# Moving the relu between the two query/key projections ahead of the same slot's exponential on ScalarE

## The chip, the core and the metric

The kernel runs on one core of a Trainium2 chip. The metric is the device time of one execution in microseconds (us); before the change it is 1559.29 us, the median of three runs that lie between 1557.75 and 1560.46 us.

## What is computed

The input is 32 images of 128 channels by 56 x 56 pixels, float32. A first layer normalises each image in groups of 4 channels, gates every channel by a small deformable convolution over the channel means and adds the result to the image. The second layer is a local attention over the result, and it is where nearly all the time goes:

```python
value = _conv1x1(x, v_w, v_b)
keyf  = _proj(x, k1_w, ..., k2_w, ...)      # 1x1 conv, batch norm, relu, twice
query = _proj(x, q1_w, ..., q2_w, ...)      # the same with other weights
uk = concatenate([_unfold3(keyf, d) for d in (1, 2, 4)])
uv = concatenate([_unfold3(value, d) for d in (1, 2, 4)])
sim = softmax(sum(uk * query))              # 27 neighbours of each pixel
out = _conv1x1(sum(sim * uv), w_w, w_b)
```

`_proj` is the part that the change touches: `h = relu(W1 x + b1)`, then `relu(W2 h + b2)`. Queries and keys are made together, 64 channels each, stacked to 128 rows.

## The kernel before

An image is cut into 7 vertical strips, 8 pixels wide, of 448 pixels each. A strip is 7 units of 8 x 8 pixels, and two units together (128 pixels) are a **tile** of the attention; an image has 25 tiles. For a tile the scores against the 256 pixels around it are one matrix product; a mask keeps the neighbours that count.

The program of each engine is written out as a list of **slots**, one for each image n and tile t, 32 x 25 of them after a ramp. The engines run through their lists in order and wait for each other by semaphores. In slot t the work of several tiles stands side by side, each at another stage:

- TensorE (PE): the scores of tile t (L416, into ps_s), the transposes of tile t-3 (L428, into ps_t), in some slots a first projection (L466, into ps_p) and the values (L489, into ps_v), then the context products of tile t-5 (L449 and L454, into ps_o), in some slots a second projection (L471, into ps_p), and small products of the normalisation of a later image.
- VectorE (DVE): the reciprocal of tile t-1's sum (L937), mask and minimum of tile t (L929), the scaling of tile t-1 (L943 or L946), statistics and small steps for later images (L982 to L1028, with L1008 waiting for GpSimd's hat_sum), the final sum of a finished strip (L954), and the values' bias (L967).
- ScalarE (ACT): the copy of a pair of transposed tiles out of PSUM (L599, into eT; every second slot), the exponential of tile t with its row sum (L584), in some slots the relu after the first projection (L634, into hid), in some slots keys and queries (L621 into kk, L610 into qq), and now and then a step for a later image (L645, L650).

The projections of the next image are laid over the current one by a table, `G_SLOT = [-10, -6, -3, 1, 4, 8, 11]`: entry g is the slot, counted from the strip's own image's slot 0, in which strip g is projected. Negative entries are the slots 15, 19 and 22 of the image ahead. So in slots 15, 19, 22, 1, 4, 8 and 11 of every image PE does a first projection and ACT the relu, and in the slot after each, 16, 20, 23, 2, 5, 9 and 12, PE does the second projection, and ACT the keys and queries.

The waits that matter here are these. The relu waits for the first projection (`h_ps`); the second projection waits for the relu (`h_done`); keys and queries wait for the second projection (`qk_ps`). The exponential of tile t waits for its masked scores (`z_done`), and the next reciprocal on DVE, which stands ahead of the mask of tile t+1, waits for the exponential (`e_done`). The context products of tile t-5 wait for the copies into eT (`eT_done`). The scores of tile t wait for the mask of tile t-2, since ps_s has two banks. ps_p and hid are single buffers.

Of the kernel before, what the change touches and what calls it, by code (L numbers as in the profile page):

```python
# [46 lines left out]
G_SLOT = [-10, -6, -3, 1, 4, 8, 11]  # L47
# [14 lines left out]
def half_tile(h):  # L62

    return divmod(h, UNITS)


def last_tile(s):

    return (UNITS * s + UNITS - 1) // 2
# [75 lines left out]
def lagged(n, t, lag):  # L145

    return (n, t - lag) if t >= lag else (n + -1, t - lag + TILES)


def slots(first, last, drain=0, register=None):  # L150

    for o in range(first, last + 1):
        for t in range(TILES):
            yield Image(o, register), t
    for t in range(drain):
        yield Image(last + 1, register), t


def build(nc, x, par, w1, w2, wv, wo, bo, bv, wg, out):
    with ExitStack() as ctx:  # L160
# [141 lines left out]
        def items_at(n, t):  # L302

            for m, rel in ((n, t), (n + 1, t - TILES)):
                if m.exists():
                    yield m, rel

        def chain_at(n, t):

            for m, rel in ((n + 1, t + TILES), (n + 2, t), (n + 3, t - TILES)):  # L310
                if m.exists():
                    yield m, rel
# [7 lines left out]
        def col(c, n=1):  # L320
            return g1[:, c:c + n]

        def images(first, last, drain=0, register=None):

            with nc.Block() as block:
# [244 lines left out]
                @block.scalar  # L570
                def _(act):
                    act.wait_ge(v_zero, 2)
                    for to in (qq[:].rearrange("p a b -> p (a b)"), kk[:].rearrange("p a b -> p (a b)"),
                               xb[:, PAIRS - 1, CHUNKS // 2, 1, :]):
                        nc.scalar.activation(to, zero[:].to_broadcast([P, to.shape[1]]),
                                             ACT.Copy).then_inc(a_zero, 1)
                    act.wait_ge(g_zs, 1)
                    act.wait_ge(a_zero, 2)

                    def exponentials(n, t):  # L580
                        i = t % RING
                        act.wait_ge(z_done.sem, z_done.count(n, t + 1))
                        act.wait_ge(rz_done.sem, rz_done.count(n, t + 1 - RING))
                        nc.scalar.activation(e[:, i, :], e[:, i, :], ACT.Exp, bias=zmin[:, i:i + 1], scale=-1.0,  # L584
                                             accum_out=zs[:, i:i + 1]).then_inc(e_done.next(), 1)

                    def copy(n, j):
                        last = min(2 * j + 1, TILES - 1)
                        act.wait_ge(t_done.sem, t_done.count(n, last + 1))

                        h = 4 * j
                        s = half_tile(h)[0]
                        if s >= ESTRIPS:
                            act.wait_ge(c_done.sem, c_done.count(n, 2 * j + 2 - ESTRIPS * UNITS // 2))
                        else:
                            act.wait_ge(c_done.sem, c_done.count(n + -1, min(TILES, 2 * j + 2 + ESTRIPS * UNITS // 2)))
                        base = 2 * UPIX * (h % (ESTRIPS * UNITS))
                        size = 4 * 2 * UPIX if last == 2 * j + 1 else 2 * UPIX
                        nc.scalar.activation(eT[:, base:base + size], ps_t[(EPAIRS * n.parity() + j) % 2][:, 0:size],  # L599
                                             ACT.Copy).then_inc(eT_done.next(), 1)  # L600

                    def queries(m, g):
                        act.wait_ge(qk_ps.sem, qk_ps.count(m, g + 1))
                        act.wait_ge(s_done.sem, s_done.count(m + -1, last_tile(g) + 1))
                        src = ps_p[0:HD, 0:SPIX].rearrange("p (u k) -> p u k", k=UPIX)
                        first = UNITS * g // 2
                        for b in range(2):
                            units = range((b + g) % 2, UNITS, 2)
                            at = (UNITS * g + units[0]) // 2
                            last = nc.scalar.activation(  # L610
                                qq[HD * b:HD * (b + 1), at:at + len(units), UPIX * b:UPIX * (b + 1)],
                                src[:, units[0]:UNITS:2, :], ACT.Relu, bias=bn_t[0:HD, 1:2])
                        last.then_inc(q_done.next(), 1)

                    def keys(m, g):
                        act.wait_ge(qk_ps.sem, qk_ps.count(m, g + 1))
                        act.wait_ge(s_done.sem, s_done.count(m + -1, last_tile(min(g + 1, STRIPS - 1)) + 1))
                        a = kk[0:HD, g, HALO * SIDE + HALO:HALO * SIDE + HALO + 1]
                        to = bass.AP(a.tensor, a.offset, [list(a.ap[0]), [BPIX - HALO, 2], [SIDE, H], [1, HALO]])
                        src = ps_p[HD:P, 0:SPIX].rearrange("p (r h c) -> p h r c", h=2, c=HALO)  # L620
                        nc.scalar.activation(to, src, ACT.Relu, bias=bn_t[HD:P, 1:2]).then_inc(k_done.next(), 1)  # L621

                    def slot(n, t):
                        m, k = lagged(n, t, TRANSPOSE)
                        if m.exists() and (k % 2 == 1 or k == TILES - 1):
                            copy(m, k // 2)
                        if n.exists():
                            exponentials(n, t)
                        for m, rel in items_at(n, t):
                            for g, at in enumerate(G_SLOT):  # L630
                                if rel == at:
                                    act.wait_ge(h_ps.sem, h_ps.count(m, g + 1))
                                    act.wait_ge(qk_ps.sem, qk_ps.count(m, g))
                                    nc.scalar.activation(hid[:], ps_p[:, 0:SPIX], ACT.Relu,  # L634
                                                         bias=b1x[:, m.parity():m.parity() + 1]).then_inc(h_done.next(), 1)
                                if rel == at + 1:
                                    keys(m, g)
                                    queries(m, g)
                        for m, at in chain_at(n, t):
                            if at == CH["a4"]:  # L640

                                act.wait_ge(dg.sem, dg.count(m, 10))
                                act.wait_ge(pg.sem, pg.count((m + -1), 13))
                                for k in range(TAPS):
                                    nc.scalar.activation(hats[:, k, 0, :], iota_f[:], ACT.Abs, bias=col(POS + k),  # L645
                                                         scale=-1.0).then_inc(ag.next(), 1)
                            if at == CH["a6"]:

                                act.wait_ge(dg.sem, dg.count(m, 11))
                                nc.scalar.activation(col(EX), col(ZS), ACT.Exp, bias=nbd[:, 0:1],  # L650
                                                     scale=-1.0).then_inc(ag.next(), 1)

                    for n, t in slots(first, last, drain, register):
                        slot(n, t)
# [436 lines left out]
```

## Time and profile before

| | |
|---|---|
| median of 3 runs | 1559.29 us (1557.75 to 1560.46) |
| the profiled execution's own time | 1560.12 us |
| its span, first to last instruction | 1558.4 us |
| granted TensorE clock, mean | 0.997 of full speed |
| busy, share of the span | PE 95%, PE weight loads 78%, DVE 77%, ACT 75%, POOL 49% |
| DMA | mean 132 GB/s |

Time of the profiled execution outside its span is 1560.12 - 1558.4 = 1.7 us. An engine's busy time counts instructions that compute; waiting is the idle time ahead of an instruction, and the view of waits names the instruction that ended it. The matmuls of this kernel are recorded in two rows each, and a timeline row merges instructions of one group that follow each other; a duration of such a row includes the end of the pipeline, so the distance between the starts of two rows says more than the durations.

### The profile page before, as it was taken

To read this page: it belongs to the slowest core of one execution; us is meant where nothing else is said; L and a number is where in the kernel's file an instruction comes from. 1 tells how busy PE (TensorE), PEld (TensorE's weight loads), DVE (VectorE), ACT (ScalarE), POOL (GpSimd) and SP (SyncE) were. 2 spreads that over 40 slices of the span, in tenths; PEclk is the share of its full clock that TensorE was granted. 3 is DMA by queue.
4 is the path that set the end of the run, shared out by engine and by line. 5 is a ranking of instruction groups with operands and counts; after the bars stand their busy time and mean duration, and the time that the engine had idled before them with its cause. 6 is when DMAs were issued, how large, how long until landed. Compare 5 with 4: busy or idle time off the path is not lost.

```text
span 1558.4 us, 35493 instructions
## 1 busy us (share of the span) xinstructions
PE 1485.3 (95%) x9287; PEld 1208.7 (78%) x9287; DVE 1204.3 (77%) x4620; ACT 1166.1 (75%) x3044; POOL 771.1 (49%) x2194
## 2 busy tenths in 40 slices
PE   1899999999999999999999999999999999999998
PEld 1588777878777778778778778778778778778886
DVE  6487778777777877778777778877778877778776
ACT  2477777777777777777777777777777777777775
POOL 6454455554455454455454555454555454555430
PEclk9999999999999999999999999999999999999999
DMA  3144553444543444553444543444543444543334
GB/s 130 37 114 150 156 159 109 137 115 148 157 140 122 135 123 147 159 144 117 134 124 147 159 143 118 136 123 146 160 141 117 137 124 146 159 143 116 97 82 137
DMA packets 104276, 205.98 MB, mean 132 GB/s; under 512 B 13584, under 2 KB 83600, under 8 KB 95888
## 3 DMA queue, kind: packets, MB, share of 16 engines
q1 hardware_dynamic: 104080, 203.72, 43.8%
q8 instruction: 80, 1.31, 0.4%
q14 instruction: 116, 0.95, 0.2%
HBM read 51.62 MB, written 51.38 MB: 66 GB/s over the span
## 4 chain that ended last, share of the span: by engine, by line
PE 72%; POOL 9%; issue 7%; DVE 6%; ACT 5%; DMA 1%; SPq 0%; ACTq 0%; POOLq 0%; DVEq 0%
PE ps_s L416 17%; PE ps_o L449 13%; PE ps_p L471 10%; PE ps_v L489 10%; PE ps_t L428 8%; PE ps_p L466 8%; POOL hats L752 5%; PE ps_o L454 2%; ACT hid L634 2%; POOL hats L751 2%; DVE e L929 1%; ACT e L584 1%; DVE e L946 1%; POOL hat_sum L755 1%; DVE rz L937 1%
## 5 line engine op out<-in xcount | busy, mean ns | idle before, releaser
L584 ACT ACTIVATE e<-e,zmin 128x256 f32<-128x256 f32 x800 | 404.4, 506 | 237.2 <-DVE zmin L929 229.4
L929 DVE CUSTOM_DVE_ANT_0 e<-ps_s,mask 128x256 f32<-128x256 f32 x800 | 334.3, 418 | 136.4 <-PE ps_s L416 129.7
L449 PEld LDWEIGHTS ps_o<-eT,v 128*128 128x128 f32 x2688 | 377.8, 191 | 74.2 <-issue 69.6
L449 PE MATMUL ps_o<-eT,v 128*128 128x128 f32 x2688 | 433.9, 276 | 0.5 <-ACT eT L599 0.3
L416 PE MATMUL ps_s<-kk,qq 128*128 128x256 f32 x1408 | 428.1, 386 | 1.5 <-DVE zmin L929 1.5
L428 PE MATMUL ps_t<-ident,e 128*128 128x128 f32 x1600 | 306.0, 273 | 0.2 <-DVE e L946 0.2
L428 PEld LDWEIGHTS ps_t<-ident,e 128*128 128x128 f32 x1600 | 225.3, 141 | 81.1 <-DVE e L946 0.5
L599 ACT ACTIVATE eT<-ps_t 128x512 f32<-128x512 f32 (+1 forms) x416 | 234.2, 563 | 48.9 <-PE ps_t L428 46.4
L416 PEld LDWEIGHTS ps_s<-kk,qq 128*128 128x128 f32 x1408 | 221.3, 192 | 37.7 <-issue 29.2
L946 DVE SCALAR_TENSOR_TENSOR e<-e,rz,keep 128x256 f32<-128x256 f32 x480 | 245.8, 512 | 0.1
L471 PE MATMUL ps_p<-hid,w2T 128*128 128x448 f32 x448 | 216.9, 566 | 27.4 <-ACT hid L634 25.8
L489 PE MATMUL ps_v<-wvox,xb 128*128 128x128 f32 x1600 | 216.9, 276 | 0.8 <-DVE v L967 0.8
L489 PEld LDWEIGHTS ps_v<-wvox,xb 128*128 128x128 f32 x1600 | 200.5, 193 | 14.6 <-issue 13.5
L937 DVE RECIPROCAL rz<-zs 128x1 f32<-128x1 f32 x800 | 124.9, 156 | 109.7 <-ACT e L584 108.4
L466 PE MATMUL ps_p<-raw,w1x 128*128 128x448 f32 x448 | 207.7, 546 | 0.9 <-ACT qq L610 0.8
L733 POOL TENSOR_TENSOR g<-g,mhalf 128x1 f32<-128x1 f32 x64 | 36.4, 569 | 340.1 <-DVE g L995 241.3
L610 ACT ACTIVATE qq<-ps_p,bn_t 64x256 f32<-64x256 f32 (+1 forms) x448 | 198.1, 442 | 8.4
L800 POOL TENSOR_SCALAR raw<-raw,g 128x448 f32<-128x448 f32 x224 | 165.0, 739 | 35.2 <-PE ps_p L466 35.2
L621 ACT ACTIVATE kk<-ps_p,bn_t 64x448 f32<-64x448 f32 x224 | 141.4, 631 | 50.1 <-PE ps_p L471 37.6
L751 POOL TENSOR_SCALAR hats<-hats 128x128 f32<-128x128 f32 x96 | 30.8, 320 | 252.7 <-ACT hats L645 247.1
L634 ACT ACTIVATE hid<-ps_p,b1x 128x448 f32<-128x448 f32 x224 | 138.3, 617 | 17.3 <-PE ps_p L466 17.2
L584 ACT ACTIVATION_READ_ACCUMULATOR e<-e,zmin 128x1 f32 x800 | 150.4, 188 | 0.0
(147 smaller groups left out, 1927.6 us busy)
## 6 DMA issues: line engine op xcount, KB each, us to landing
raw<-in_x_dram SPq DMA_DIRECT2D x32, 1568.0 KB, 7.3
out_dram<-raw SPq DMA_DIRECT2D x32, 1568.0 KB, 5.4
v<-v SPq DMA_DIRECT2D x192, 224.0 KB, 3.2
kk<-kk SPq DMA_DIRECT2D x192, 112.0 KB, 2.2
ksp<-kk SPq DMA_DIRECT2D x192, 64.0 KB, 2.5
v<-v_last SPq DMA_DIRECT2D x64, 128.0 KB, 2.9
kk<-kk SPq DMA_DIRECT2D x32, 224.0 KB, 2.9
v<-v_last SPq DMA_DIRECT2D x64, 96.0 KB, 2.7
```

What stands on the lines that cost most here:

```text
L416: nc.tensor.matmul(ps_s[i][:, 0:KEYS].rearrange("p (s h k) -> p h s k", s=2, h=2), qq[:, t, :], window.rearrange("p h (s k) -> p h s k", s=2),
L428: last = nc.tensor.transpose(o[:, base:base + KEYS].rearrange("p (a s k) -> p s a k", a=2, s=2)[:, i], e[:, t % RING, P * i:P * (i + 1)], ...
L449: last = nc.tensor.matmul(o[:, UPIX * (u - 1):UPIX * (u + 1)], v[:, s, u, :], eT[:, UPIX * (base + 2 * u - 1):UPIX * (base + 2 * u + 1)], ...
L466: nc.tensor.matmul(ps_p[:, 0:SPIX].rearrange("p (r c) -> p r c", c=SIDE), w1x[:, m.parity(), :], strip_of(m, g), start=True, stop=True).th ...
L471: nc.tensor.matmul(ps_p[:, 0:SPIX], w2T[:], hid[:], start=True, stop=True).then_inc(qk_ps.next(), 1)
L489: last = nc.tensor.matmul(ps_v[:, P * j:P * (j + 1)], pixels, wvox[:, m.parity(), :], start=True, stop=True)
L584: nc.scalar.activation(e[:, i, :], e[:, i, :], ACT.Exp, bias=zmin[:, i:i + 1], scale=-1.0, accum_out=zs[:, i:i + 1]).then_inc(e_done.next( ...
L599: nc.scalar.activation(eT[:, base:base + size], ps_t[(EPAIRS * n.parity() + j) % 2][:, 0:size], ACT.Copy).then_inc(eT_done.next(), 1)
L610: last = nc.scalar.activation(qq[HD * b:HD * (b + 1), at:at + len(units), UPIX * b:UPIX * (b + 1)], src[:, units[0]:UNITS:2, :], ACT.Relu, ...
L634: nc.scalar.activation(hid[:], ps_p[:, 0:SPIX], ACT.Relu, bias=b1x[:, m.parity():m.parity() + 1]).then_inc(h_done.next(), 1)
L929: nc.vector.tensor_tensor_reduce(e[:, i, :], ps_s[(TILES * n.parity() + t) % 2][:, 0:KEYS], mask[:].rearrange("p s h a b -> p (s h a b)"), ...
L946: nc.vector.scalar_tensor_tensor(e[:, i, :], e[:, i, :], rz[:, i:i + 1], keep[:, KINDS.index(outside(t)), :], ALU.mult, ALU.mult).then_inc ...
```

## The change

In ACT's slot the relu between the two projections is issued ahead of the exponential of the same slot. The copy before it, and the keys and queries behind it, stay where they were. No instruction is added or removed, and the other engines' lists are the same.

```diff
                         if m.exists() and (k % 2 == 1 or k == TILES - 1):
                             copy(m, k // 2)
-                        if n.exists():
-                            exponentials(n, t)
                         for m, rel in items_at(n, t):
                             for g, at in enumerate(G_SLOT):
                                 if rel == at:
                                     act.wait_ge(h_ps.sem, h_ps.count(m, g + 1))
                                     act.wait_ge(qk_ps.sem, qk_ps.count(m, g))
                                     nc.scalar.activation(hid[:], ps_p[:, 0:SPIX], ACT.Relu,
                                                          bias=b1x[:, m.parity():m.parity() + 1]).then_inc(h_done.next(), 1)
+                        if n.exists():
+                            exponentials(n, t)
+                        for m, rel in items_at(n, t):
+                            for g, at in enumerate(G_SLOT):
                                 if rel == at + 1:
                                     keys(m, g)
                                     queries(m, g)
```

Two lines are added to the file above L634, so lines behind them have other numbers in the changed kernel: the relu is L632 there, the steps L645 and L650 are L647 and L652.

ACT's list from slot 21 to slot 24 of image 0, before (e, zs is the exponential of a tile, hid the relu, eT the copy, kk and qq the keys and queries, hats a step for a later image):

```order
L584 ACTIVATE e,zs<-e,zmin 128x256
L645 ACTIVATE hats<-iota_f,g 128x128 x3
L599 ACTIVATE eT<-ps_t 128x512
L584 ACTIVATE e,zs<-e,zmin 128x256
L634 ACTIVATE hid<-ps_p,b1x 128x448
L584 ACTIVATE e,zs<-e,zmin 128x256
L621 ACTIVATE kk<-ps_p,bn_t 64x2x56x4
```

And with the change:

```order
L584 ACTIVATE e,zs<-e,zmin 128x256
L647 ACTIVATE hats<-iota_f,g 128x128 x3
L599 ACTIVATE eT<-ps_t 128x512
L632 ACTIVATE hid<-ps_p,b1x 128x448
L584 ACTIVATE e,zs<-e,zmin 128x256 x2
L621 ACTIVATE kk<-ps_p,bn_t 64x2x56x4
```

In slot 22 the relu now follows the copy at once, and the exponential of tile 22 comes behind it, directly ahead of that of tile 23.

Slots 1 and 2 of the image after, ACT, before:

```order
L599 ACTIVATE eT<-ps_t 128x512
L584 ACTIVATE e,zs<-e,zmin 128x256
L634 ACTIVATE hid<-ps_p,b1x 128x448
L599 ACTIVATE eT<-ps_t 128x128
L584 ACTIVATE e,zs<-e,zmin 128x256
```

And with the change:

```order
L599 ACTIVATE eT<-ps_t 128x512
L632 ACTIVATE hid<-ps_p,b1x 128x448
L584 ACTIVATE e,zs<-e,zmin 128x256
L599 ACTIVATE eT<-ps_t 128x128
L584 ACTIVATE e,zs<-e,zmin 128x256
```

Here the relu of strip 3 and the exponential of tile 1 have changed places. The other five slots with a relu change in the same way.

## Rows read from the trace of the kernel before

**Rows 1.** The page's first part: busy us, share of the span, instructions

```profile
PE 1485.3 (95%) x9287; PEld 1208.7 (78%) x9287; DVE 1204.3 (77%) x4620; ACT 1166.1 (75%) x3044; POOL 771.1 (49%) x2194
```

**Rows 2.** View of waits, whole span: us in total, times, longest us

```profile
DVE e L929 <- PE ps_s L416: 129.7, 255, 2.1
...
PEld ps_p L471 <- ACT hid L634: 41.9, 66, 2.2
...
PE ps_p L471 <- ACT hid L634: 25.8, 36, 1.8
```

**Rows 3.** Timeline, PE, slot 20 of one image: start us, us, instruction, count, [idle]

```profile
707.09 0.61 PE L449 MATMUL ps_o<-eT,v 128*128 128x128 f32 x4
707.54 0.92 PE L471 MATMUL ps_p<-hid,w2T 128*128 128x448 f32 x2
```

**Rows 4.** Timeline, all engines, slots 15 and 16, rows of PE and ACT

```profile
743.97 0.92 PE L466 MATMUL ps_p<-raw,w1x 128*128 128x448 f32 x2
...
745.31 0.51 ACT L584 ACTIVATE e<-e,zmin 128x256 f32<-128x256 f32 x1 [0.65 <-DVE zmin L929]
...
745.82 0.61 PE L449 MATMUL ps_o<-eT,v 128*128 128x128 f32 x4
746.48 1.02 PE L471 MATMUL ps_p<-hid,w2T 128*128 128x448 f32 x2
```

**Rows 5.** Timeline, PE, slots 23 to 2 around an image's start

```profile
712.78 0.61 PE L449 MATMUL ps_o<-eT,v 128*128 128x128 f32 x4
713.24 1.02 PE L471 MATMUL ps_p<-hid,w2T 128*128 128x448 f32 x2
...
716.52 0.71 PE L449 MATMUL ps_o<-eT,v 128*128 128x128 f32 x4
...
717.95 0.92 PE L466 MATMUL ps_p<-raw,w1x 128*128 128x448 f32 x2
...
719.58 0.61 PE L449 MATMUL ps_o<-eT,v 128*128 128x128 f32 x4
720.91 1.02 PE L471 MATMUL ps_p<-hid,w2T 128*128 128x448 f32 x2 [0.72 <-ACT hid L634]
```

**Rows 6.** Timeline, all engines, slots 19, 20 and 23, rows of ACT and DVE

```profile
705.69 0.51 ACT L584 ACTIVATE e<-e,zmin 128x256 f32<-128x256 f32 x1 [1.16 <-DVE zmin L929]
...
706.20 0.63 ACT L634 ACTIVATE hid<-ps_p,b1x 128x448 f32<-128x448 f32 x1
...
707.07 0.42 DVE L929 CUSTOM_DVE_ANT_0 e<-ps_s,mask 128x256 f32<-128x256 f32 x1 [0.55 <-PE ps_s L416]
...
712.85 0.42 DVE L929 CUSTOM_DVE_ANT_0 e<-ps_s,mask 128x256 f32<-128x256 f32 x1
```

**Rows 7.** Timeline, ACT, slots 22 to 2

```profile
711.60 0.58 ACT L599 ACTIVATE eT<-ps_t 128x512 f32<-128x512 f32 x1
712.08 0.50 ACT L584 ACTIVATE e<-e,zmin 128x256 f32<-128x256 f32 x1
...
712.57 0.62 ACT L634 ACTIVATE hid<-ps_p,b1x 128x448 f32<-128x448 f32 x1
713.32 0.51 ACT L584 ACTIVATE e<-e,zmin 128x256 f32<-128x256 f32 x1
...
714.30 0.63 ACT L621 ACTIVATE kk<-ps_p,bn_t 64x448 f32<-64x448 f32 x1 [0.38 <-PE ps_p L471]
...
715.87 0.60 ACT L599 ACTIVATE eT<-ps_t 128x512 f32<-128x512 f32 x1
...
719.73 0.51 ACT L584 ACTIVATE e<-e,zmin 128x256 f32<-128x256 f32 x1 [0.77 <-DVE zmin L929]
...
720.24 0.61 ACT L634 ACTIVATE hid<-ps_p,b1x 128x448 f32<-128x448 f32 x1
720.76 0.27 ACT L599 ACTIVATE eT<-ps_t 128x128 f32<-128x128 f32 x1
```

## The prediction

> **What bounds the kernel now.** I read the page's busy shares first. PE is busy for 95% of the span, ACT and DVE for 75% and 77% [rows 1]. So PE is the engine to follow, and a change on ACT is worth what it takes out of PE's waits or puts into them.
>
> The view of waits says who makes PE wait. The second projection (L471) waits for the relu (L634) 36 times for 25.8 us, and its weight load 66 times for 41.9 us [rows 2]; 36 + 66 = 102 events are about three in each of 32 images. In the other direction DVE waits 129.7 us for PE's scores [rows 2]: over a whole image the softmax loop on DVE and ACT has time to spare, about 129.7 / 32 = 4.1 us.
>
> The timeline then tells which three slots these are, and what each costs. Seen in slot 20, where nothing waits, the second projection starts 707.54 - 707.09 = 0.45 us after the four context products ahead of it [rows 3]. Against this I hold the slots that do wait:
>
> - Slot 16: 746.48 - 745.82 = 0.66 us [rows 4], 0.21 late.
> - Slot 23: 713.24 - 712.78 = 0.46 us, 0.01 late.
> - Slot 2: 720.91 - 719.58 = 1.33 us, 0.88 late [rows 5].
>
> In all three the second projection's row is also 1.02 us long and not 0.92 [rows 3 to 5]: its weights could not be loaded ahead of time, and I count the 0.10 us as PE time too. That makes 0.31, 0.11 and 0.98 us, **1.40 us of PE time per image**. In slots 5, 9, 12 and 20 the projection does not wait, so an earlier relu gives nothing there.
>
> **The change part by part.** Nothing is added or removed; on ACT a relu and an exponential change places in seven slots per image. ACT issues no DMA, so no queue is passed.
>
> *The relu, earlier.* It can start when its first projection is over and ACT is free.
> Slot 15: the first projection ends at 743.97 + 0.92 = 744.89, and ACT is idle from 745.31 - 0.65 = 744.66 [rows 4]. The relu, 0.62 us long [rows 7], is over by 745.55; the second projection is wanted at 745.82 + 0.45 = 746.27. The 0.31 us go entirely. From here PE leads by 0.31.
> Slot 22: the relu takes the place of the exponential at 712.08 and is over at 712.70 instead of 713.19 [rows 7]. With PE 0.31 ahead the projection is wanted at 713.23 - 0.31 = 712.92. The 0.11 us go; the lead is 0.42.
> Slot 1: the first projection ends at 717.95 + 0.92 = 718.87 [rows 5], ACT is idle from 719.73 - 0.77 = 718.96 [rows 7]. The relu could be over by 719.6 instead of 720.85, and the projection is wanted at 719.58 + 0.45 = 720.03 on the old clock. Here the relu waited for an exponential that itself waited for DVE. The 0.98 us go.
>
> *The exponential, later.* A relu pushes what stands behind it by 720.76 - 720.24 = 0.52 us [rows 7], plus any time that ACT now idles until the projection is over.
> Slot 19 is the bad one. The exponential runs at 705.69, while PE is still in the first projection, and the relu follows at 706.20 [rows 6]. Swapped, the relu stays where it is, or 0.31 earlier with PE's lead, at 705.89, and the exponential comes at 706.41 instead of 705.69, 0.72 later. The next mask on DVE, where it waits for nothing else, follows an exponential after 712.85 - 712.08 = 0.77 us [rows 6, 7], so here at 707.18. It stood at 707.07, having waited 0.55 for PE [rows 6]. That slack hides all but 0.11 us.
> Slot 22: copy and relu come 0.1 late, the exponential of tile 22 at 712.08 + 0.10 + 0.52 = 712.70. The next one follows after 713.32 - 712.08 = 1.24 us [rows 7], a round of exponential, reciprocal, mask, exponential: at 713.94. Keys come 712.57 - 712.08 = 0.49 behind it [rows 7], at 714.43. They stood at 714.30, where they waited for the second projection [rows 7]; that is no longer what ends last. The keys, the queries and the copy of the next pair into eT keep their distance of 715.87 - 714.30 = 1.57 us [rows 7], so the copy starts at 716.00, 0.13 later than before.
> **That copy is what is late next.** The context products of slot 0 start at 716.52, 0.65 behind it, and their row is 0.71 us against 0.61 elsewhere [rows 3, 5]: they already wait for it a little. PE arrives there with a lead of 0.42 and now finds the copy 0.13 later than before: the lead is lost, and 0.13 with it, 0.55 us in all.
> Slot 1 then has everything 0.13 later: the first projection ends at 719.00, the relu at about 719.66, and the second projection is wanted at 720.16. It still doesn't wait.
> Slots 4, 8, 11 and 15: the exponential there moves by 0.5 to 0.6 us at most, and the next mask is one that waits for PE's scores, as in slot 20 (0.55 us [rows 6]); I cost them at nothing. If that cover is thinner than in slot 20, each costs up to 0.1 us, as slot 19 does.
>
> *The sum.* 1.40 - 0.55 = 0.85 us per image. Of the 32 images the first starts in the ramp and the last has no next image to project; I count 30, so 0.85 x 30 = 25 us. The profiled execution took 1560.12 us and would take 1535; it stands 0.8 us above the median of the runs, so the forecast is 1559.3 - 25 = **1534 us**.
>
> The uncertain term is the 0.55. Its lower end is 0: if keys still follow the second projection directly, the copy moves with PE and nothing is lost. Its upper end, from the rows, is a full 0.72 of slot 19 and 0.62 of slot 22 passed on, 1.34 at the copy, plus the lead of 0.42: 1.76. I take 0.55, near the lower end, because the wait in slot 20 that hides most of the 0.72 is in the rows.
>
> The relu's 0.62 us and 0.52 to the next start are this trace's [rows 7]. The Trainium skill's page "ScalarE: Activation LUTs", section "What ACT_TABLE_LOAD costs", gives an ACTIVATE with a per-partition bias about 280 ns + 0.833 ns per element and an overlap of 93 ns with the next: an estimate from it is 653 ns for 448 elements and 0.56 us to the next start. By that each push would be 0.04 us longer, the copy 0.08, and the sum 2.4 us smaller, 1536 us; the rows are measured here and decide.
>
> **The rivals.**
>
> *All of it comes out.* If the late exponentials are caught up before slot 0, the full 1.40 x 30 = 42 us are gained: 1517 us. For it: the 4.1 us per image that DVE waits. Against: the copy ahead of slot 0 is reached by the chain of slots 19 to 24, where only slot 20 has a wait to give.
>
> *The wait turns into another and the time stays, or gains little.* PE meets a later copy, or scores whose mask is late, and gives back 1 to 1.4 of the 1.40 us: 1547 to 1559 us. The Trainium skill speaks for this in "Perfetto Trace Analysis", section "Identifying the Most-Contended Engine": matmul busy time is no good measure of how full TensorE is, the weight loads' share is better, and that share is 78% here [rows 1], no more than DVE's. By that rule the loop on DVE and ACT would set the pace and the time would stay at 1559 us. The 129.7 us that DVE waits for PE [rows 2] speak against it.
>
> *Slower: ACT stands idle in front of a relu while a ready exponential waits behind it.* The place is slot 19, 0.72 us, followed by slot 22, 0.62. If both reach the copy before slot 0, PE loses 1.76 and gains 1.40: 0.36 x 30 = 11 us, 1570 us. It decides from 1.40 - 0.42 = 0.98 us of delay at the copy on. For it: ACT is strictly in order, and the mask of the next tile stands behind the reciprocal that needs the exponential. Against: the 0.55 us in slot 20.
>
> That the relu isn't earlier at all is true in slot 19 alone, where it starts at the projection's end already.
>
> **How the numbers follow.** The forecast, with the 0.55 off by 0.25 either way (1526 to 1542 us), has 0.55. All of it, down to 1515, has 0.13. A small gain, 1542 to 1556, has 0.12. No change has 0.09, slower 0.11. A measurement of this kernel tells about 0.2%, 3 us, from no change, so faster is 0.55 + 0.13 + 0.12 = 0.80. The range from 1515 to 1556 us leaves out no change and slower, 0.20. The likeliest case's own range is 1526 to 1542.
>
> **What would show it.** In the profile after, the wait of the second projection for the relu should be nearly gone, 41.9 and 25.8 us down to a few. PE's context products of slot 0 should wait for the copy into eT, about 0.5 us per image, some 15 us in all where there were almost none. The exponential should stand behind the relu in seven slots, and DVE's wait for PE's scores should fall by 10 us or more, most of it in slot 20. Keys in slot 23 should wait for ACT's exponential and no longer for PE. I am wrong if the scores (L416) or transposes (L428) start to wait for DVE, or if the relu still ends last in slot 2.

## The result, and the profile after

The changed kernel takes **1550.8 us** (median of 6 runs, 1548.23 to 1555.5) and the kernel before, beside it, 1559.88 us (6 runs, 1557.75 to 1560.97). The ratio is 0.9945 with a 95% interval of 0.9934 to 0.9956. So 9.1 us are gained where 25 were forecast: the sign was right, the size was not, and 1550.8 lies inside the range only through the case "a small gain".

The page's first part of the changed kernel, whose profiled execution took 1550.79 us with a span of 1549.1 us at the same granted clock of 0.997:

```profile
PE 1481.5 (96%) x9287; PEld 1203.9 (78%) x9287; DVE 1198.9 (77%) x4620; ACT 1175.4 (76%) x3044; POOL 779.1 (50%) x2194
```

The busy times moved by about 1% at most against [rows 1]; the gain is waiting time. The view of waits of the changed kernel (us in total, times, longest us):

```profile
DVE rz L939 <- ACT e L584: 192.4, 352, 1.6
...
DVE e L931 <- PE ps_s L416: 42.7, 97, 1.1
...
PEld ps_o L449 <- ACT eT L599: 24.0, 38, 0.7
...
PE ps_o L449 <- ACT eT L599: 14.9, 30, 0.5
...
PEld ps_p L466 <- ACT qq L610: 12.9, 33, 0.9
...
PEld ps_p L471 <- ACT hid L632: 5.0, 4, 2.1
...
PE ps_p L471 <- ACT hid L632: 2.2, 4, 0.7
```

The wait for the relu is all but gone: 41.9 and 25.8 us in [rows 2], 5.0 and 2.2 now. Two waits have come in its place. The context products (L449) wait for the copy into eT, 30 times 0.5 us. And the first projection's weight load (L466) waits 33 times for the queries (L610), 31 of them in slot 4, once per image; that one stood in no row of the prediction. DVE waits 42.7 us for PE's scores where it was 129.7 [rows 2], and in exchange longer for the exponential, 192.4 us (108.4 before).

To see where in an image the time went, I take the distance from the start of one scores row (L416) on PE to the next as the length of a slot, and the median over images 2 to 28. An image fell from 46.73 to 46.42 us, by 0.32 of unrounded times; 0.32 x 30 = 9.6 us, close to the 9.1 us measured. All the difference lies in five slots:

| slot | before | after | difference | forecast |
|---|---|---|---|---|
| 16 | 2.17 | 1.85 | -0.31 | -0.31 |
| 23 | 1.97 | 1.90 | -0.07 | -0.11 |
| 0 | 1.43 | 2.09 | +0.66 | +0.55 |
| 2 | 2.98 | 1.99 | -0.99 | -0.98 |
| 4 | 2.74 | 3.13 | +0.39 | 0 |

These slots can be read off one image. Timeline of PE in the kernel before, slots 0 to 4 (start us, us, instruction, count); the five starts of scores bound slots 0, 1, 2 and 4:

```profile
715.86 0.60 PE L416 MATMUL ps_s<-kk,qq 128*128 128x256 f32 x2
...
717.30 0.60 PE L416 MATMUL ps_s<-kk,qq 128*128 128x256 f32 x2
...
718.92 0.60 PE L416 MATMUL ps_s<-kk,qq 128*128 128x256 f32 x2
...
721.90 0.68 PE L416 MATMUL ps_s<-ksp,qq 128*128 128x256 f32 x2
...
723.08 0.60 PE L416 MATMUL ps_s<-kk,qq 128*128 128x256 f32 x2
723.52 0.38 PE L428 MATMUL ps_t<-ident,e 128*128 128x128 f32 x2
723.74 0.92 PE L466 MATMUL ps_p<-raw,w1x 128*128 128x448 f32 x2
...
725.83 0.60 PE L416 MATMUL ps_s<-kk,qq 128*128 128x256 f32 x2
```

The timeline of the same image after, PE and its weight loads, from slot 23 on:

```profile
708.62 0.61 PE L449 MATMUL ps_o<-eT,v 128*128 128x128 f32 x4
709.07 0.97 PE L471 MATMUL ps_p<-hid,w2T 128*128 128x448 f32 x2
...
711.64 0.60 PE L416 MATMUL ps_s<-kk,qq 128*128 128x256 f32 x2
712.08 0.38 PE L428 MATMUL ps_t<-ident,e 128*128 128x128 f32 x2
712.96 0.71 PE L449 MATMUL ps_o<-eT,v 128*128 128x128 f32 x4 [0.50 <-ACT eT L599]
...
713.73 0.60 PE L416 MATMUL ps_s<-kk,qq 128*128 128x256 f32 x2
...
715.36 0.60 PE L416 MATMUL ps_s<-kk,qq 128*128 128x256 f32 x2
...
717.35 0.68 PE L416 MATMUL ps_s<-ksp,qq 128*128 128x256 f32 x2
...
718.53 0.60 PE L416 MATMUL ps_s<-kk,qq 128*128 128x256 f32 x2
718.97 0.38 PE L428 MATMUL ps_t<-ident,e 128*128 128x128 f32 x2
719.48 0.30 PEld L466 LDWEIGHTS ps_p<-raw,w1x 128*128 128x128 f32 x2 [0.37 <-ACT qq L610]
719.48 1.02 PE L466 MATMUL ps_p<-raw,w1x 128*128 128x448 f32 x2
...
721.67 0.60 PE L416 MATMUL ps_s<-kk,qq 128*128 128x256 f32 x2
```

Slot 2 is now 717.35 - 715.36 = 1.99 us instead of 2.98. Slot 0 is 713.73 - 711.64 = 2.09 instead of 1.44, with the wait for eT inside. In slot 4 the first projection starts 719.48 - 718.97 = 0.51 us behind the transposes; before it was 723.74 - 723.52 = 0.22. Its weights come late as well, so its row is 1.02 us long and not 0.92: 0.29 + 0.10 = 0.39 us, the slot's whole loss. With the distance between the two traces at the scores of slot 14 as zero, PE's lead in this image is 0.31 us after slot 16, 0.37 at the start of slot 0, minus 0.28 after it, 0.70 after slot 2 and 0.30 after slot 4.

The gain of slot 16, on PE of the next image (before: [rows 4]):

```profile
741.66 0.61 PE L449 MATMUL ps_o<-eT,v 128*128 128x128 f32 x4
742.11 0.92 PE L471 MATMUL ps_p<-hid,w2T 128*128 128x448 f32 x2
```

The second projection starts 0.45 us behind the context products and its row is 0.92 us long, as in a slot where nothing waits.

ACT's timeline after, of the same image, tells whom PE waits for:

```profile
702.03 0.64 ACT L632 ACTIVATE hid<-ps_p,b1x 128x448 f32<-128x448 f32 x1 [1.66 <-PE ps_p L466]
702.57 0.50 ACT L584 ACTIVATE e<-e,zmin 128x256 f32<-128x256 f32 x1
...
708.35 0.61 ACT L632 ACTIVATE hid<-ps_p,b1x 128x448 f32<-128x448 f32 x1
708.87 0.50 ACT L584 ACTIVATE e<-e,zmin 128x256 f32<-128x256 f32 x1
...
710.11 0.51 ACT L584 ACTIVATE e<-e,zmin 128x256 f32<-128x256 f32 x1 [0.65 <-DVE zmin L931]
...
710.73 0.63 ACT L621 ACTIVATE kk<-ps_p,bn_t 64x448 f32<-64x448 f32 x1
...
712.31 0.60 ACT L599 ACTIVATE eT<-ps_t 128x512 f32<-128x512 f32 x1
...
717.25 0.51 ACT L584 ACTIVATE e<-e,zmin 128x256 f32<-128x256 f32 x1 [0.57 <-DVE zmin L931]
...
717.87 0.63 ACT L621 ACTIVATE kk<-ps_p,bn_t 64x448 f32<-64x448 f32 x1
718.53 0.90 ACT L610 ACTIVATE qq<-ps_p,bn_t 64x192 f32<-64x192 f32 x2
```

In slot 19 (the first two rows) ACT stands idle for 1.66 us ahead of the relu, with the exponential behind it; the exponential's masked scores are complete at 701.49, 0.54 us before the relu starts. The keys of slot 23 follow the exponential of tile 23 (710.11) and no longer the projection, and the copy at 712.31 is the one that the context products of slot 0 wait for: 712.96 - 712.31 = 0.65, as before. The queries of strip 3 end at 718.53 + 0.90 = 719.43, and at 719.48 the first projection of strip 4 begins. It writes ps_p, the single buffer that the queries read; the queries stand behind the keys, and these behind the exponential of tile 2 at 717.25, which waited for DVE.

### The profile page after: what moved, and what is told of

The parts are those of the page before. It is cut to its first block, busy times and chain, and to the rows that moved or that the text cites. A ratio compares the mean times of both kernels' runs of the same rounds, so it can differ in the third digit from the quotient of the medians.

```text
span 1549.1 us, 35493 instructions
## 1 busy us (share of the span) xinstructions
PE 1481.5 (96%) x9287; PEld 1203.9 (78%) x9287; DVE 1198.9 (77%) x4620; ACT 1175.4 (76%) x3044; POOL 779.1 (50%) x2194
## 4 chain that ended last, share of the span: by engine, by line
PE 61%; DVE 13%; issue 10%; POOL 8%; ACT 7%; DMA 1%; SPq 0%; ACTq 0%; POOLq 0%; DVEq 0%
PE ps_s L416 14%; PE ps_o L449 12%; PE ps_p L466 9%; PE ps_v L489 8%; PE ps_t L428 7%; PE ps_p L471 6%; POOL hats L754 4%; PE ps_o L454 2%; DVE e L931 2%; ACT e L584 2%; POOL hats L753 2%; ACT hats L647 2%; DVE e L948 2%; DVE cells L1003 1%; ACT kk L621 1%
## 5 line engine op out<-in xcount | busy, mean ns | idle before, releaser
L449 PEld LDWEIGHTS ps_o<-eT,v 128*128 128x128 f32 x2688 | 377.8, 191 | 93.8 <-issue 69.6
L449 PE MATMUL ps_o<-eT,v 128*128 128x128 f32 x2688 | 434.1, 276 | 15.2 <-ACT eT L599 14.9
L416 PE MATMUL ps_s<-kk,qq 128*128 128x256 f32 x1408 | 428.1, 386 | 1.5 <-DVE zmin L931 1.5
L931 DVE CUSTOM_DVE_ANT_0 e<-ps_s,mask 128x256 f32<-128x256 f32 x800 | 333.9, 417 | 50.0 <-PE ps_s L416 42.7
L939 DVE RECIPROCAL rz<-zs 128x1 f32<-128x1 f32 x800 | 126.2, 158 | 193.6 <-ACT e L584 192.4
L599 ACT ACTIVATE eT<-ps_t 128x512 f32<-128x512 f32 (+1 forms) x416 | 234.9, 565 | 25.8 <-PE ps_t L428 23.3
L416 PEld LDWEIGHTS ps_s<-kk,qq 128*128 128x128 f32 x1408 | 221.3, 192 | 37.6 <-issue 29.4
L948 DVE SCALAR_TENSOR_TENSOR e<-e,rz,keep 128x256 f32<-128x256 f32 x480 | 237.4, 495 | 0.1
L632 ACT ACTIVATE hid<-ps_p,b1x 128x448 f32<-128x448 f32 x224 | 141.6, 632 | 110.8 <-PE ps_p L466 107.7
L466 PE MATMUL ps_p<-raw,w1x 128*128 128x448 f32 x448 | 211.3, 554 | 4.9 <-ACT qq L610 1.3
L471 PE MATMUL ps_p<-hid,w2T 128*128 128x448 f32 x448 | 209.1, 549 | 2.2 <-ACT hid L632 2.2
L610 ACT ACTIVATE qq<-ps_p,bn_t 64x256 f32<-64x256 f32 (+1 forms) x448 | 198.0, 442 | 8.4
L802 POOL TENSOR_SCALAR raw<-raw,g 128x448 f32<-128x448 f32 x224 | 171.8, 769 | 35.0 <-PE ps_p L466 35.0
```

What stands on the lines that cost most here:

```text
L416: nc.tensor.matmul(ps_s[i][:, 0:KEYS].rearrange("p (s h k) -> p h s k", s=2, h=2), qq[:, t, :], window.rearrange("p h (s k) -> p h s k", s=2),
L449: last = nc.tensor.matmul(o[:, UPIX * (u - 1):UPIX * (u + 1)], v[:, s, u, :], eT[:, UPIX * (base + 2 * u - 1):UPIX * (base + 2 * u + 1)], ...
L466: nc.tensor.matmul(ps_p[:, 0:SPIX].rearrange("p (r c) -> p r c", c=SIDE), w1x[:, m.parity(), :], strip_of(m, g), start=True, stop=True).th ...
L471: nc.tensor.matmul(ps_p[:, 0:SPIX], w2T[:], hid[:], start=True, stop=True).then_inc(qk_ps.next(), 1)
L610: last = nc.scalar.activation(qq[HD * b:HD * (b + 1), at:at + len(units), UPIX * b:UPIX * (b + 1)], src[:, units[0]:UNITS:2, :], ACT.Relu, ...
L802: gp.tensor_scalar(to, to, col(X_A + m.offset % RAWS), col(X_B + m.parity()), ALU.mult, ALU.add).then_inc(x1_done.next(), 1)
```

## The experiments

Three theories were set against each other.

- **A, two named waits.** The relu of slots 15 and 1 gives its full gain. What takes it back is (1) the exponentials of slots 19 and 22, pushed behind their relus, which make the copy ahead of slot 0 late, and (2) in slot 4 the queries that still hold ps_p, a wait that the late relu of slot 2 had covered.
- **B, the loop.** The softmax loop on DVE and ACT sets the pace, and any lead that PE wins is taken back somewhere.
- **C, the copies of keys.** PE ahead of time meets the DMA into ksp (the copy of the keys that some scores read) in slot 10.

All variants name the strips whose relu is issued first, and put the rest back behind the exponential. A variant's cut shows the lines in which it differs from the kernel before or from a variant already shown. Strips 0 to 6 stand for slots 15, 19, 22, 1, 4, 8 and 11:

```diff
+RELU_FIRST = (0, 3)
...
-                                if rel == at:
+                                    if rel == at and (g in RELU_FIRST) == where:
...
+                        relu(True)
                         if n.exists():
                             exponentials(n, t)
+                        relu(False)
+                        keys_queries(False)
```

The line numbers of the variants are 2 to 22 higher than in the changed kernel.

### Only slots 15 and 1

> The relu goes first in slots 15 and 1 alone (strips 0 and 3); in slots 19, 22, 4, 8 and 11 the exponential goes first, as before the change. Theory A (two named waits: the exponentials pushed in slots 19 and 22 make the copy into eT late in slot 0, and the first projection of slot 4 finds ps_p still read by the queries of slot 2): the context products of slot 0 no longer wait for the copy more than before; PE gains 0.31 + 0.98 us per image and gives back about 0.5 in slot 4: 0.8 x 30 = 24 us, 1535 us. Theory B (the softmax loop of DVE and ACT sets the pace, and PE's lead is taken back whichever slots are swapped): about the time of the change, 1550 us.

Measured: 1544.05 us, ratio 0.9896 (0.9883 to 0.9909) to 1560.27 us. The view of waits:

```profile
PEld ps_p L468 <- ACT qq L612: 20.4, 33, 0.9
...
PE ps_p L468 <- ACT qq L612: 12.4, 31, 0.8
...
PEld ps_o L451 <- ACT eT L601: 1.8, 6, 0.5
```

With slots 19 and 22 put back the wait for eT is gone (14.9 and 24.0 us in the changed kernel), and the time is better than the whole change's. But the loss in slot 4 grew from 0.39 to 0.66 us per image: the two waits had partly covered each other. In the changed kernel PE came out of slot 0 0.28 us late, and the exponential of tile 2, on which the queries hang, did not come later with it: it starts 25.82 us behind the scores of slot 14 there (median over images 2 to 28), 25.80 before the change. Here PE is not late, and the whole 0.66 shows. A's 1535 had 0.5 for it and was missed by 9 us, of which this is 5; B's 1550 was missed too.

### Only slots 19 and 22

```diff
-RELU_FIRST = (0, 3)
+RELU_FIRST = (1, 2)
```

> The relu goes first in slots 19 and 22 alone (strips 1 and 2). Theory A: nothing but the harm is left: the copy ahead of slot 0 comes about 0.45 us later than before the change and PE waits for it, less the 0.1 us of slot 23: 0.35 to 0.45 us per image, 10 to 13 us, 1570 us. Theory B: no place to gain, none to lose, 1557 to 1560 us.

Measured: 1569.31 us, ratio 1.0064 (1.0051 to 1.0077). The view of waits:

```profile
PEld ps_o L451 <- ACT eT L601: 23.2, 36, 0.7
...
PE ps_o L451 <- ACT eT L601: 14.7, 30, 0.5
```

The wait of slot 0 stands here alone, at the size that it has in the changed kernel, and slot 0 is 0.65 us longer. This half of the change is a loss of 9 us. B had no loss here.

### Only slot 1

```diff
-RELU_FIRST = (0, 3)
+RELU_FIRST = (3,)
```

> The relu goes first in slot 1 alone (strip 3). Theory A: 0.98 us gained in slot 2, about 0.55 given back in slot 4 by the first projection waiting for the queries: 0.4 x 30 = 13 us, 1547 us, and the row of that wait about 0.5 us per image. Theory B: PE's lead goes somewhere else too, 1555 to 1560 us.

Measured: 1549.16 us, ratio 0.9928 (0.9916 to 0.994). Slot 2 gains its 0.99 us and slot 4 gives 0.65 back, though slot 4's own relu stands where it stood before the change: the loss comes with PE's lead out of slot 2. B's 1555 to 1560 is missed. One moved relu of the seven is worth as much as all seven together.

### The whole change, and in slot 4 the values ahead of the first projection

To take away the wait in slot 4, PE does the value products, which don't touch ps_p, before the first projection of strip 4:

```diff
+VALUES_FIRST = (4,)
...
-                                if rel == at:
+                                if rel == at and g not in VALUES_FIRST:
                                     hidden(m, g)
                             if rel in V_SLOT:
                                 values(m, V_SLOT.index(rel))
+                            for g, at in enumerate(G_SLOT):
+                                if rel == at and g in VALUES_FIRST:
+                                    hidden(m, g)
```

> The change as it is, all seven slots swapped, and on PE in slot 4 the eight value products ahead of the first projection instead of behind it, so that the projection wants ps_p about 0.9 us later. Theory A: the wait for the queries goes and 0.39 us per image with it, 12 us against the change, 1539 us; the wait of slot 0 for the copy stays at 0.5 us. Theory B: the wait turns up in another place, 1550 us.

Measured: 1552.16 us, ratio 0.9956 (0.994 to 0.9972), no better than the change alone. The wait for the queries did go (1.4 us), but another came. The view of waits:

```profile
PEld ps_s L419 <- DMA ksp<-kk: 25.8, 33, 2.3
...
PE ps_s L419 <- DMA ksp<-kk: 11.0, 8, 1.7
```

In 6 of 27 images the scores of slot 10 wait some 1.5 us more for the keys' copy, and the mean image is 46.55 us long where the median is 46.25 (in the changed kernel 46.52 and 46.42). The relu of slot 4 stands ahead of the exponential here and comes later than in the changed kernel, since its projection does; it pushes the exponential, and the keys of strip 4 end 2.78 us behind the scores of slot 5 instead of 2.46. So the wait that C names is there, in one combination. That the later keys bring it is not shown: in those six images the copy takes 5.8 to 6.1 us from issue to landing, 4.1 in the median image, and such copies also occur where the keys are on time (slots 4, 8 and 11 alone, below).

### Slots 15 and 1, and in slot 4 the values first

```diff
+RELU_FIRST = (0, 3)
+VALUES_FIRST = (4,)
```

> The relu first in slots 15 and 1 alone, and on PE the value products of slot 4 ahead of its first projection. The run before it with seven slots swapped moved keys of strip 4 by 0.3 us, because the relu of slot 4, now later, pushed the exponential; here that relu stays behind the exponential. Theory A: the 0.66 us that slot 4 costs with these two slots swapped falls to 0.2 or less, and nothing else grows: 0.45 x 30 = 13 us against that run, 1530 us. Theory C (past slot 5 PE meets the transfer of the keys, ksp, which the scores of slot 10 wait for, so that slot 4's wait only protected it): 1542 to 1546 us, with the wait for ksp up by 10 us or more.

Measured: 1532.44 us, ratio 0.9823 (0.9806 to 0.9839) to 1560.06 us. With the relu of slot 4 left behind its exponential the copy of the keys is no obstacle: PE's weight loads wait 8.2 us for it in all (6.0 before the change), and C's 1542 us or more is missed. 27.6 us are gained, near the 25 that I had forecast for the whole change. Slot 4 is still 0.40 us longer than before, for a new reason. Its timeline:

```profile
708.24 0.38 PE L431 MATMUL ps_t<-ident,e 128*128 128x128 f32 x2
708.38 0.15 DVE L1033 TENSOR_TENSOR g<-g,ps_v 128x1 f32<-128x1 f32 x1
...
708.79 1.13 PE L492 MATMUL ps_v<-wvox,xb 128*128 128x128 f32 x8 [0.16 <-issue]
```

The values start 0.55 us behind the transposes. They write ps_v, and PE's program holds them until a step of the normalisation on DVE that reads ps_v (L1033) is over. The row names no instruction as releaser, but in every image from 2 to 28 they start 0.25 us behind the end of that step, while their distance from the transposes varies from 0.53 to 0.64. One buffer was exchanged for another.

### Only slot 19

> The relu first in slot 19 alone. The exponential of tile 19 is pushed by about 1.0 us, of which DVE's wait of 0.55 hides half: copy, relu and second projection of slots 22 and 23 come about 0.4 us later, PE waits there, nothing is gained: 0.4 x 30 = 12 us, 1571 us. If the push is hidden entirely: 1559 us.

```diff
+RELU_FIRST = (1,)
```

Measured: 1573.25 us, ratio 1.008 (1.0064 to 1.0096). The view of waits:

```profile
PEld ps_p L473 <- ACT hid L635: 54.8, 94, 2.2
```

The late exponential of slot 19 makes the next ones late, and the relu of slot 22, still behind its exponential, with them. The second projection of slot 23 waits for it: 41.9 us [rows 2] become 54.8, and slot 23 is 0.42 us longer.

### Only slot 22

> The relu first in slot 22 alone. PE gains 0.1 us in slot 23; the exponential of tile 22 is pushed by 0.62 us, the keys of slot 23 and the copy behind them by 0.13, and the context products of slot 0 wait 0.24 longer; slot 2's wait shrinks by the 0.13, since the exponential there does not move: about 0, 1557 to 1562 us. If the push is passed on whole: 0.6 us in slot 0, 1570 us or more.

```diff
+RELU_FIRST = (2,)
```

Measured: 1558.96 us, ratio 0.9991 (0.9979 to 1.0002): no change that can be told. Slot 0 loses 0.27 us; slots 2 and 23 give 0.25 and 0.11.

### Only slots 4, 8 and 11

> The relu first in slots 4, 8 and 11 alone. The prediction costs these at nothing: every slot of PE keeps its length, 1558 to 1562 us. If the cover there is thinner: up to 0.1 us per slot and image, 9 us in all, 1569 us.

```diff
+RELU_FIRST = (4, 5, 6)
```

Measured: 1563.44 us, ratio 1.002 (1.0011 to 1.0029), slower by 3.4 us where nothing was expected. No slot's median moves, but the mean image is 46.93 us against a median of 46.72. The view of waits:

```profile
PEld ps_s L418 <- DMA ksp<-kk: 8.9, 12, 1.8
...
PE ps_s L418 <- DMA ksp<-kk: 3.2, 3, 1.1
```

In 3 of the 27 images the scores of slot 10 wait 1.0 to 1.1 us for the copy of the keys, and slot 9 is 1.2 us longer by it: 3.7 us in all, the whole loss. Before the change the mean image is 46.81 against 46.73. The keys and the issue of the copy come at the same times as before; in these three images the copy lands after 5.9 to 6.0 us, where the longest was 5.0. Why is open, and one profiled execution can't tell whether the swap brings it.

### Slots 15 and 1, and in slot 4 the context products first

PE's slot 4 has three pieces besides scores and transposes: first projection, values, context products. The last two variants order them freely, here as context, values, first projection:

```diff
+LATE = (2, 1, 0)
...
+                        parts = (first_projections, value_products, contexts)
+                        for part in LATE if t == G_SLOT[4] else (0, 1, 2):
+                            parts[part]()
```

> The relu first in slots 15 and 1 alone, and on PE in slot 4 the order is context products, value products, first projection. In the run with the value products ahead slot 4 still cost 0.40 us, of which the value products' wait for a normalisation step on DVE, 0.3 us, is the larger part. The context products need 0.44 us and would cover it. Theory A: slot 4 costs 0.1 us or less: 0.3 to 0.4 x 30 = 9 to 12 us against that run, 1521 to 1523 us. Theory C (the transfer of ksp ends last in slot 10): 1530 us or more, the wait for ksp up by 8 us or more.

Measured: 1526.82 us, ratio 0.9769 (0.9755 to 0.9782) to 1561.57 us. Slot 4 has its old length again, though slot 5 loses 0.11. A's 1521 to 1523 is missed by 4 us: slot 5 makes 3.4 of it, and in 2 of 27 images the scores of slot 10 wait 1.0 us for the keys' copy.

And as context, first projection, values:

```diff
-LATE = (2, 1, 0)
+LATE = (2, 0, 1)
```

> The same with the order context products, first projection, value products in slot 4: the projection wants ps_p 0.44 us later than in the run with two relus moved and no change on PE, and 0.9 minus 0.44 earlier than with the value products ahead. Theory A: of the 0.66 us in slot 4 some 0.22 stay: 0.44 x 30 = 13 us against that run, 1531 us.

Measured: **1525.12 us**, ratio 0.9768 (0.9755 to 0.9782), with the first of these two the fastest of the study; between the two nothing is told. The view of waits of the second:

```profile
DVE e L953 <- PE ps_s L419: 89.0, 197, 1.0
...
PEld ps_p L469 <- ACT qq L623: 2.3, 4, 0.9
```

The context products cover the wait for the queries. DVE still waits 89.0 us for PE's scores: the loop has room even at 1525 us. With its three forecasts missed B falls as the limit of the whole kernel; between the masks of tiles 1 and 2, though, DVE is not idle for a moment (images 2 to 28, before the change and after it), and there the loop does set when ps_p comes free. The time is 6 us below A's 1531. Of these 0.15 us per image, 4.6 us, come from slot 8, where small products of the normalisation start 0.15 us earlier; that was not forecast, and what releases them is open.

The slots that differ from the kernel before, us per image:

| variant | 0 | 2 | 4 | 16 | 23 | image |
|---|---|---|---|---|---|---|
| the change | +0.66 | -0.99 | +0.39 | -0.31 | -0.07 | 46.42 |
| 15 and 1 | | -0.99 | +0.66 | -0.31 | | 46.10 |
| 19 and 22 | +0.65 | -0.25 | | | -0.07 | 47.06 |
| 1 | | -0.99 | +0.65 | | | 46.38 |
| 19 | | | | | +0.42 | 47.14 |
| 22 | +0.27 | -0.25 | | | -0.11 | 46.63 |
| the change, values first | +0.65 | -0.99 | +0.14 | -0.31 | -0.07 | 46.25 |
| 15 and 1, values first | | -0.99 | +0.40 | -0.31 | | 45.82 |
| 4, 8 and 11 | | | | | | 46.72 |
| 15 and 1, context, values first | | -0.99 | | -0.31 | | 45.56 |
| 15 and 1, context first | | -0.99 | +0.22 | -0.31 | | 45.51 |

"The change, values first" has 0.21 more in slot 7 and 0.28 less in slot 8 besides, the row above the last 0.11 more in slot 5, the last row 0.15 less in slot 8. These are medians: the few images that wait for the copy of the keys show in the means alone.

## Why the prediction was right in sign and wrong in size

**What bounds the kernel: right, with one view misread.** PE is the engine to follow: the gains and losses stand in the slots where PE's waits went or came, and the difference of the mean image, times 30, gives each measured difference to within 3 us. PE's busy share went from 95% to 97% in the fastest variant. The "102 events" are not three waits per image: 93 of them are slot 2 counted twice, once for the matmul and once for its weight load, and the weight load of slot 16, 31 times each; slot 23's 0.11 us is in the timeline alone. The three slots and their prices came from the timeline and stand.

The Trainium skill says in "Perfetto Trace Analysis", section "Identifying the Most-Contended Engine", that the weight loads' share, and not the matmuls' busy time, tells how near TensorE is to its peak. That the softmax loop would then set the pace and the time stay at 1559 us was my own inference, and it failed: that share was 78% before and after, DVE's 77%, and the time fell with PE's waits. The share did not tell here whose waits set the time.

**The relu, earlier: right, to 0.05 us.** Slots 16, 23 and 2 gave 0.31, 0.07 and 0.99 against 0.31, 0.11 and 0.98. In slot 23 the relu ends at 708.35 + 0.61 = 708.96, so close to the projection at 709.07 that its weights are still a little late: its row is 0.97 long and not 0.92.

**The exponential, later, and the copy ahead of slot 0: the mechanism right, the size 0.11 short.** At the scores of slots 14 and 15 the two traces are 3.85 us apart; with that added, on the old clock, the exponentials of slots 19 and 23 start at 706.42 and 713.96; forecast were 706.41 and 713.94. The keys start at 714.58 instead of 714.43, and the copy at 716.16 instead of 716.00, which is 0.29 later than before and not 0.13. With the lead of 0.37 (715.86 - 3.85 - 711.64) that makes the 0.66 of slot 0. The wrong step is "Keys come 712.57 - 712.08 = 0.49 behind it": that row is a relu's. Keys need 0.62 (710.11 to 710.73, 717.25 to 717.87), and ACT's timeline before the change had it:

```profile
693.88 0.50 ACT L584 ACTIVATE e<-e,zmin 128x256 f32<-128x256 f32 x1
...
694.50 0.63 ACT L621 ACTIVATE kk<-ps_p,bn_t 64x448 f32<-64x448 f32 x1
```

**"Slots 4, 8, 11 and 15 ... I cost them at nothing": the step that failed.** I asked there only what the pushed exponential does to the next mask, and that does cost nothing in the median image (slots 4, 8 and 11 alone). I did not ask what PE meets in slot 4 when it comes 0.99 us early out of slot 2; the sum has no term for it. It meets ps_p: the keys and queries that must empty it hang on an exponential, and that on DVE's masks, not on PE. The old wait for the relu had hidden this. It costs 0.39 us per image, and 0.65 with slot 1's relu moved alone. Of the miss of 0.85 - 0.32 = 0.53, slot 4 has 0.39, slot 0 has 0.11 and slot 23 has 0.04.

The Trainium skill says in "Perfetto Trace Analysis", section "Matmuls", that independent groups of matmuls should rotate through different PSUM banks, so that emptying one overlaps with filling the next. The wait in slot 4 agrees with it: the first projection's weight load waits 33 times, 12.9 us, for the queries to empty ps_p. A second buffer for ps_p wasn't tried.

**The rivals.** "The wait turns into another" gave 1547 to 1559 us, and it is what happened, though through a buffer that I had not named. "Slower" had its place right: slots 19 and 22 by themselves cost 9 us. Its price was too high: with both pushes slot 0 loses 0.66, not 1.76. "All of it comes out" fell with the waits in slots 0 and 4, and the 4.1 us per image that DVE waited did not prevent them.

**The signs to look for** came as said but for one: the relu's wait is gone, PE waits 14.9 us with the context products, the exponential stands behind the relu, the keys of slot 23 follow the exponential, and neither scores nor transposes wait longer for DVE. DVE's wait for PE's scores fell by 87 us, but not most of it in slot 20: that slot had 16.8 us of it, and slots 3, 12, 24, 17 and 9 gave up 9 to 20 us each. None of the signs could have shown slot 4, since none asked about L466.

## What to carry to other kernels

When a wait goes away, follow the engine that won the lead to its next use of every single buffer, and price each with the time at which it is released in the old trace: the second-latest wait in a slot becomes its bound. A lead won long before can move that release too: with the relu of slots 15 and 1 first, the exponential of tile 2 starts 25.50 us behind the scores of slot 14 and not 25.80. An order that helps in one place of a list can harm in another, so try the places apart: here two of seven gave all but 0.07 us of the gain, and with one piece of PE's work put over the next wait they gave 36 us instead of 9. Take the distance between two instructions from rows of the same pair, not from a similar one.

## What the runs showed of the hardware that was not expected

On ACT the next instruction starts 0.49 to 0.56 us behind the start of an exponential where it is a relu or a copy and nothing holds it, but 0.61 to 0.63 where it is the keys' ACTIVATE over 64 partitions. What makes the difference was not tried apart.

The copies of the keys into ksp, all of one size, land after very different times. In the changed kernel the view of the tile ksp gives, from issue to landing:

```profile
DMA to landing us min/median/max: 2.0/2.6/5.9
```

Most of this spread goes by place: of an image's six copies the two of strip 4 take 4.9 and 3.9 us in the median image, the others 2.0 to 2.6. The tail is in the second of these two, 5.9 us in one image of the changed kernel against its usual 3.9. So a kernel can have a few images that wait for such a copy while the median image doesn't; the variant of slots 4, 8 and 11 is 0.2% slower, and three such images account for it.
